# Fourier stage of a four-layer image network: in the first shared tick of a slot, the first widening matmuls stand ahead of the first output product

## What is computed

```python
def _L2_conv_ref(x, w_in, w_dw, fft_filter, w_out):
    x = jnp.einsum('bchw,oc->bohw', x, w_in)              # 64 -> 384 channels
    xp = x.reshape(B, C, H // 8, 8, W // 8, 8).transpose(0, 1, 2, 4, 3, 5)
    xf = jnp.fft.rfft2(xp) * fft_filter                   # per channel, per frequency
    xp = jnp.fft.irfft2(xf, s=(8, 8))
    x = xp.transpose(0, 1, 2, 4, 3, 5).reshape(B, C, H, W)
    x = lax.conv_general_dilated(x, w_dw, ..., feature_group_count=C)   # 3 x 3, per channel
    x1, x2 = jnp.split(x, 2, axis=1)
    x = jax.nn.gelu(x1, approximate=False) * x2
    return jnp.einsum('bchw,oc->bohw', x, w_out)          # 192 -> 64 channels
```

## Time and profile before

| | us |
|---|---|
| median of 3 runs (21081.33 to 21089.35) | 21081.68 |
| the profiled execution, its time | 21098.81 |
| the profiled execution, span of its instructions | 21097.0 |
| whole span: DVE busy | 19421.3 (92%) |
| whole span: POOL busy | 15394.4 (73%) |
| whole span: PE busy | 14907.7 (71%) |
| whole span: ACT busy | 11474.3 (54%) |
| Fourier stage, 17168 to 20720: DVE, POOL, PE, ACT busy | 3065.3, 3026.9, 2849.9, 2156.3 |

### The profile page before, as it was taken

One profiled execution on the slowest core, in us unless ns is written; L12 is line 12 of the kernel. 1 busy time (PEld: TensorE's weight loads), 2 busy tenths in 40 slices (PEclk: granted clock), 3 DMA queues, 4 the chain that ended last, 5 costly groups with the idle time before them and its releaser, 6 DMA issues. The chain is left out here.

```text
span 21097.0 us, 183109 instructions
## 1 busy us (share of the span) xinstructions
PE 14907.7 (71%) x47074; PEld 5387.9 (26%) x47074; DVE 19421.3 (92%) x12666; ACT 11474.3 (54%) x12716; POOL 15394.4 (73%) x6584
## 2 busy tenths in 40 slices
PE   4876666666666666666666666666666668888885
PEld 2331222222222222222222222222222224444444
DVE  5778999999999999999999999999999978888886
ACT  1115555555555555555555555555555546666663
POOL 3766777777777777777777777777777758888881
PEclk8887777777777777777777777777777779999997
DMA  3224444444444444444444444444444421111113
GB/s 117 95 90 112 111 114 116 111 113 116 114 109 116 115 112 114 115 112 112 114 117 110 114 116 110 114 116 114 109 116 114 111 63 30 30 30 30 30 26 132
DMA packets 574458, 2089.44 MB, mean 99 GB/s; under 512 B 70785, under 2 KB 88051, under 8 KB 550067
## 3 DMA queue, kind: packets, MB, share of 16 engines
q1 hardware_dynamic: 569122, 2081.45, 39.6%
q10 hardware_dynamic: 5265, 7.14, 0.1%
HBM read 856.39 MB, written 158.18 MB: 48 GB/s over the span
## 5 line engine op out<-in xcount | busy, mean ns | idle before, releaser
L1287 POOL TENSOR_TENSOR prod<-h,c_bc 128x1024 f32<-128x1024 f32 x4096 | 9571.1, 2350 | 4069.1 <-PE py L992 3088.1
L1246 DVE TENSOR_TENSOR_SCAN h<-da,state,px 128x1024 f32<-128x1024 f32 x4096 | 9613.4, 2347 | 193.2 <-DVE px L1239 24.6
L1133 ACT ACTIVATE da<-d_bc,a_neg 128x1024 f32<-128x1024 f32 x4096 | 4666.6, 1145 | 4670.2 <-DVE h L1246 4644.1
L1239 DVE TENSOR_TENSOR px<-px,du_bc 128x1024 f32<-128x1024 f32 x4096 | 5046.0, 1232 | 359.6 <-PE px L925 141.2
L925 PE MATMUL px<-cf,bsel 32*128 32x512 f32 x4096 | 3113.4, 899 | 3199.0 <-DVE h L1246 3198.9
L992 PE MATMUL py<-prod,ysel 128*32 128x512 f32 x16384 | 2725.9, 798 | 1560.0 <-POOL prod L1287 1560.0
L1874 POOL TENSOR_TENSOR acc<-acc,ta 128x1024 f32<-128x1024 f32 (+1 forms) x1040 | 2424.7, 2339 | 499.7 <-DVE acc L1774 370.1
L925 PEld LDWEIGHTS px<-cf,bsel 32*128 32x128 f32 x4096 | 957.5, 257 | 4989.4 <-DVE h L1246 4037.7
L1774 DVE SCALAR_TENSOR_TENSOR p_c<-zb,w_dw,p_c 128x1024 f32<-128x1024 f32 (+1 forms) x1560 | 1987.3, 1274 | 42.3 <-PE p_c L1546 9.8
L992 PEld LDWEIGHTS py<-prod,ysel 128*32 128x32 f32 x16384 | 511.2, 132 | 3808.6 <-POOL prod L1287 2800.9
L1673 ACT ACTIVATE ta<-zb,w_dw 128x1024 f32<-128x1024 f32 (+1 forms) x1040 | 1168.5, 1128 | 297.1 <-POOL acc L1874 275.5
(11 more groups left out here) (219 smaller groups left out, 18319.6 us busy)
## 6 DMA issues: line engine op xcount, KB each, us to landing
d_bc<-delta SPq DMA_DIRECT2D x1024, 512.0 KB, 8.1
du_bc<-du SPq DMA_DIRECT2D x1024, 512.0 KB, 7.7
c_bc<-c_rows_dram SPq DMA_DIRECT2D x1024, 512.0 KB, 4.0
hx<-x_dram SPq DMA_DIRECT2D x252, 256.5 KB, 4.8
st_x<-in_x_dram SPq DMA_DIRECT2D x32, 1024.0 KB, 4.8
ax<-in_x_dram SPq DMA_DIRECT2D x64, 512.0 KB, 3.4
xr<-x_dram SPq DMA_DIRECT2D x64, 512.0 KB, 6.0
x_dram<-xo SPq DMA_DIRECT2D x64, 512.0 KB, 5.3
```

The source lines that it names most:

```text
L1133: nc.scalar.activation(da[n % 4][:, :], d_bc[:, n % J, :], ACT.Exp, scale=a_neg[t.l][:, n:n + 1]).then_inc(da_done, 1)
L1239: nc.vector.tensor_tensor(out=x[:, :], in0=px[q % 2][:, :], in1=du_bc[:, j, :], op=ALU.mult).then_inc(m1_done, 1)
L1246: nc.vector.tensor_tensor_scan(h[:, n % 8, :], da[n % 4][:, :], x[:, :], state[:, 2 * t.l + t.b, n:n + 1], ALU.mult, ALU.add).then_inc(sca ...
L1287: nc.gpsimd.tensor_tensor(out=prod[j][:, :], in0=h[:, n % 8, :], in1=c_bc[q % 2][:, :], op=ALU.mult).then_inc(m2_done, 1)
```

## The change

In the PE list of every slot, the widening that falls into a tick is issued ahead of the output product of the same tick. Only tick 1 holds both, so only group 0 of each slot moves, ahead of the first product.

```diff
--- before.py
+++ after.py
@@ -1582,11 +1582,11 @@
                 for j in range(TICKS):
                     if j in CONV_AT:
                         conv(s, b, CONV_AT[j])
+                    if not no_next and j in WIDEN_AT:
+                        widen(ns, r + b, nb, WIDEN_AT[j])
                     if not first and j in PROJECT_AT:
                         project(s - 1, nb, r if rows_left else None, PROJECT_AT.index(j))
                     if not no_next:
-                        if j in WIDEN_AT:
-                            widen(ns, r + b, nb, WIDEN_AT[j])
                         if j in BACK_AT:
                             from_freq(ns, BACK_AT[j])
                         if j == NEXT_AT:
```

## The result

| | before | after |
|---|---|---|
| median of 6 runs each, us | 21083.85 (21081.33 to 21092.79) | 20990.54 (20986.09 to 20993.0) |
| ratio after / before | | 0.9955, 95% interval 0.9942 to 0.9968 |
| span of the profiled execution | 21097.0 | 20989.2 |
| DVE idle ahead of the filter, ended by the widening | 374.5 | 273.5 |

A forecast was written before the change was run, and what follows sets the result against it. DVE and PE waiting for each other in turn at slot heads set the pace. Thirty pairs going from 105.81 to 102.4, plus 2.5, less 1.3, save 103.5 us; taken off the 21081.7 median: 20978 us, range 20955 to 21015.

The forecast's parts named there:

- What bounds the stage: Slot heads: DVE and PE wait for each other in turn; DVE idles 374.5 us ahead of the filter.
- Odd slot: Odd head: the widening leads, DVE's whole 1.26 us idle goes, the product stays hidden; gain 1.25 us.
- POOL's cover: Odd slot: POOL's 1.51 us wait for DVE absorbs the 1.25 gain, leaving 0.25.
- Even slot at half clock: Even head: widening takes 1.75 us, filter starts 2.1 earlier, third filter waits about 1.1; gain 1.3 us.
- the sum: Both slots' gains with the clock as it is: a pair gains 2.55 us and takes 103.26.
- The floor: Pair with a short half-clock stretch: 101.98 us, not much less because ACT's even-slot tap waits for POOL.
- The tie at 102.4: Loop of pairs held by free-running clock drops at 102.4 us a pair, short and long stretches in turn; chance 0.60.
- The size: Whole kernel: 30 pairs x (105.81 - 102.4), plus 2.5 for first heads, less 1.3, makes 103.5 us saved.
- 1: Even heads: the long half-clock stretch stays in every pair; 79 us saved, 21003 us; chance 0.17.
- 2: Even heads: short half-clock stretch, or none, in all pairs; 117 us saved, 20964 us; chance 0.08.
- 3: Heads: the wait moves on to the residual; under 1.3 us a pair left, 21042 to 21082; chance 0.10.
- 4: Even head: more half clock, the remaining 9.7 us doubled; pair 7 us longer, 21300 us; chance 0.05.

## Why the prediction came out as it did

- **What bounds the stage: right.** DVE and PE waited for each other in turn at the heads; DVE's busy time is unchanged and only idle went. Each head alone shortens the loop.
- **Odd slot: right.** The idle of 1.26 is gone, the product stays hidden, and POOL's cover shrank from 1.51 to 0.22 (0.25 forecast).
- **Even slot at half clock: right, the widening's size a little off.** 1.65 us measured for my 1.75. The filter waits 1.71 (1.8 forecast), the third filter 1.07 (1.1), the residual not at all. The Trainium skill, "TensorE: Matmul & The Clock Gate", section on the clock gate, has half rate as the default that idle leads back to. The trace agrees in the pair with the long stretch, 1.65 instead of 0.92, and not in the third kind of pair, where the same idle of 3.73 is followed by a convolution at full clock (1.98). A pair with the long stretch takes 103.06 where the sum had 103.26.
- **The floor: right in size, its cause only in part.** Pairs with a short stretch or none take 102.11 and 102.01, forecast 101.98; the second way back waits 1.42 for ACT in the latter. But the tap that waits for POOL is not all that holds it: the placement ahead of it left pairs with a short stretch at 102.1, and took 0.48 off pairs without a long one only together with the earlier widening. What holds the 102.0 besides was not taken apart.
- **The tie at 102.4: right in its value, 102.39.** I had "short and long in turn" and drops 102.4 apart; it is long, short, none, with drops 105.8 and 201.4 apart. The step behind it, that every even head meets a drop, earlier or later, does not hold: in one pair of three there is none, after the same idle of 3.73. Added work on DVE, added work on PE and an edit of ACT's order left the mean at 102.39 to 102.41. What I had wrong of the tie is that I took 102.4 and 105.8 to be its only places. With one head changed it holds at 104.10 over two pairs, and 102.4 is reached over three pairs, over four, and in single pairs once the widening is one tick earlier.
- **The size: 103.5 forecast, 104.4 between the first and the last even head of the two profiles, 93 between the medians.** Of the 104.4, 82.1 are the last 24 pairs, 24 x 3.42, the size that the sum had for a pair. That the whole agrees to 1 us is partly luck: in three profiles of the kernel before the same stretch took 3277.1, 3281.4 and 3275.6 us. The sum was made against a profiled execution that lies 15 us above the before median of the six runs (21098.8 against 21083.85); the step from there to "20978" took that distance as a constant for both kernels. It isn't: the changed kernel's profiled execution, 20990.97, lies on its median. In the six runs each of that measurement the kernel before spreads over 11.5 us (21081.3 to 21092.8), the changed one over 7 (20986.1 to 20993.0), and over all groups the kernel before runs from 21077 to 21102. Two of its profiles show 9 us of that in the entry into the tie and ahead of the stage; whether its shorter executions are tied at all stays open. Against the other two groups' medians, 21090.9 and 21093.7, the changed kernel is 100 and 103 us faster, against the third, 21078.9, 88. That is the term that was off: the change of reference from the profiled execution to the median.
- **Rivals.** 1 describes one of the three kinds of pair, 2 the other two, and neither holds alone. 3, the wait moving to the residual, is absent here and appears with 0.96 us once the widening goes one tick earlier. 4 is out: no half-clock stretch of the loop is longer than the 6.7 us it was before.

## What to carry to other kernels

When two engines wait for each other in turn, look for the piece that stands between them and is wanted later than what stands behind it; moving the wanted piece ahead costs nothing as long as the other still comes in time, and that margin can be read from the timeline. If the pairs of a loop all take exactly the same time and PE runs at half clock somewhere in them, suspect that the clock and not the work sets the length: a piece of added work with which the pairs come out shorter shows it, and so does idle that is filled with useless work. A mean that added work leaves unchanged shows little by itself, since most of the addition can vanish in idle further on (0.20 of 0.27 us here). In such a loop small savings may show nothing until the idle that lets the clock fall is filled or removed.

## What the runs showed of the hardware that I had not expected

- A loop can tie itself to the drops of the granted clock, over one pair (105.81, and 102.40 with the widening ahead of the convolution), two (2 x 104.10), three (307.18) or four (4 x 102.41), and edits that change single pairs by a tenth of a microsecond then leave the mean where it is.
- With 0.17 us more DVE work in each, pairs took 105.38 on average, 0.43 us less than in the three profiles of the kernel before (whether for the added work or for another execution is open).
- The clock fell once in four pairs after a stretch in which PE was busy 2.00 of 3.40 us; its longest idle there was 1.40 us. An idle of 3.7 us was not needed, and in one pair of three of the changed kernel an idle of 3.73 us was not followed by a drop.
